# Second attention layer: the first mixture's outputs reach x by accumulating transfers from GpSimd

## The reference

```
x = x + graph_attention_0(layernorm(x), adj)      # 1 head
x = x + mixture_0(layernorm(x))                   # 8 experts, the best 2 of each token, weighted
x = x + graph_attention_1(layernorm(x), adj)      # 8 heads
x = x + mixture_1(layernorm(x))                   # 8 experts, the best 2 of each token, weighted
```

## Time and profile before

| | |
|---|---|
| median of 3 runs | 1700.94 us |
| the profiled execution's own time | 1694.58 us |
| its span | 1692.5 us |
| mean granted TensorE clock | 0.831 of full speed |
| last transfer issue of the first mixture, on GpSimd | 669.95 us |
| first work of the second attention layer, on GpSimd and SP | 675.76 us |
| first product with the neighbours, on TensorE | 752.47 us |

### The profile page before, as it was taken

The page is one execution under the profiler, slowest core; times in us unless marked ns, Lnnn a source line. Parts: engine busy times, 40 slices in busy tenths (PEclk is TensorE's granted clock), DMA queues, the critical chain, the costliest instruction groups (busy, mean ns, idle before and its releaser), DMA issues. The chain is left out here.

```text
span 1692.5 us, 31275 instructions
## 1 busy us (share of the span) xinstructions
PE 1099.7 (65%) x11083; PEld 1004.3 (59%) x11083; DVE 1103.8 (65%) x2450; ACT 1045.6 (62%) x1456; POOL 886.1 (52%) x694
## 2 busy tenths in 40 slices
PE   4677777731487672227777767777663169999960
PEld 3677677631376561127676667776663159999960
DVE  5689888762254441777989999999996224333424
ACT  5567766621365451059989999999981156666630
POOL 1011655686377776210312376776788626666660
PEclk9889977965699996558988898988886579999985
DMA  7654442112465550822221222322311355555528
GB/s 220 248 182 148 160 148 79 57 44 107 123 181 162 160 154 22 239 100 64 88 102 64 87 90 93 110 88 87 96 61 42 112 168 163 163 167 170 166 67 268
DMA packets 166122, 213.69 MB, mean 126 GB/s; under 512 B 29812, under 2 KB 121102, under 8 KB 164944
## 3 DMA queue, kind: packets, MB, share of 16 engines
q1 hardware_dynamic: 147792, 175.99, 33.8%
q0 software_dynamic: 18176, 35.72, 6.1%
HBM read 156.71 MB, written 58.56 MB: 127 GB/s over the span
## 5 line engine op out<-in xcount | busy, mean ns | idle before, releaser
L474 POOL DMA_INDIRECT y_dram<-f_ys,f_Xb x312 | 339.1, 1087 | 180.7 <-DVE f_ys L495 97.1
L1629 ACT ACTIVATE g_near<-g_s_row,g_steep 128x1024 fp8e4<-128x1024 f32 x400 | 420.9, 1138 | 17.0 <-issue 11.7
L185 POOL DMA_INDIRECT xs_dram<-r_row,r_pos x256 | 323.4, 1263 | 122.7 <-issue 77.2
L1573 PE MATMUL g_bp<-g_G,g_near 128*128 128x102 bf16 x4096 | 237.6, 228 | 151.1 <-DVE g_near L1439 151.0
L1573 PEld LDWEIGHTS g_bp<-g_G,g_near 128*128 128x128 fp8e4 x4096 | 229.7, 110 | 163.5 <-issue 163.3
L541 PEld LDWEIGHTS f_ops<-f_w,f_g 128*128 128x128 f32 x1872 | 239.9, 192 | 14.5 <-ACT f_g L577 0.7
L541 PE MATMUL f_ops<-f_w,f_g 128*128 128x128 f32 x1872 | 247.3, 275 | 0.1
L577 ACT ACTIVATE f_g<-f_hps,f_ex 128x512 f32<-128x512 f32 x234 | 160.8, 688 | 91.4 <-PE f_hps L533 91.1
L914 PE MATMUL attout<-V,Pt 128*128 128x129 f32 x1024 | 147.5, 305 | 28.4 <-DVE Pt L749 28.4
L1439 DVE TENSOR_TENSOR g_near<-g_near,g_mask 128x2048 uint32<-128x2048 uint32 x64 | 154.5, 2414 | 5.5 <-ACT g_near L1629 2.8
L914 PEld LDWEIGHTS attout<-V,Pt 128*128 128x128 f32 x1024 | 138.4, 217 | 29.7 <-DVE Pt L749 29.7
(11 more groups left out here) (237 smaller groups left out, 2107.3 us busy)
## 6 DMA issues: line engine op xcount, KB each, us to landing
raw<-in_adj SPq DMA_DIRECT2D x64, 512.0 KB, 6.2
g_s_row<-rows_dram SPq DMA_DIRECT2D x64, 512.0 KB, 3.8
f_Xb<-xs_dram SPq DMA_DIRECT2D x78, 288.0 KB, 3.0
f_w<-in_L_ffn_W SPq DMA_DIRECT2D x78, 256.0 KB
f_w<-in_L_ffn_W SPq DMA_DIRECT2D x78, 128.0 KB
mask_dram<-mask SPq DMA_DIRECT2D x16, 512.0 KB, 3.7
g_near<-y_dram SPq DMA_DIRECT2D x8, 1024.0 KB, 7.6
g_mask<-mask_dram SPq DMA_DIRECT2D x8, 1024.0 KB, 6.5
```

The costliest lines, as they stand in the source:

```text
L185: pool.indirect_dma_start(rows_d, bass.IndirectOffsetOnAxis(ap=pos[:, c % 2, k, t:t + 1], axis=0), row[:, c % RB, k, t, :], None, bounds_c ...
L474: pool.indirect_dma_start(y_d.rearrange("n k d -> (n k) d"), bass.IndirectOffsetOnAxis(ap=Xb[:, i % XB, r, D:D + 1].bitcast(U32), axis=0), ...
L1573: ins = pe.matmul(bp[h % 2][:, t // 4, (t % 4) * 6 * C:(t % 4 + 1) * 6 * C], near[:, k % 3, j, t * P:(t + 1) * P], G[:, s, j, h, :, :], st ...
L1629: ins = act.activation(near[:, k % 3, j, :], s_row[:, k % 3, :], ACT.Relu, scale=STEEP, bias=steep[:, s, j, h:h + 1], saturate=False)
```

## The change

The buffers for y, the eight loads and the sixteen sums on VectorE are gone, and so are the semaphore `s_add` and the waits for it. GpSimd issues two transfers for each batch, one for the first output and one for the second, which add what they read from `y_dram` to what is in `x_sb` (`accum_op=ALU.add`). The second of a batch waits for the first to land. VectorE's `take_moments(c)` waits until both have landed, and then does what the second half of `add_outputs(c)` did. Each batch has a semaphore of its own, `s_yl[c]`.

```diff
-            def load_outputs(b):
-                wait(sp, s_add, 2 * (b - 1))
-                sp.dma_start(yb[:, b % 2, :, :, :], y_d[b * N:(b + 1) * N, :, :].rearrange("(t p) k d -> p t k d", p=P)).then_inc(s_yl[b % 2], 16)
-
-            load_outputs(0)
-            load_outputs(1)
...
                     for h in range(4):
-                        if b == 0 and h == 1:
-                            for c in range(5, B):
-                                load_outputs(c)
                         load_row(b, h)
...
                 if b == -1:
-                    load_outputs(2)
-                    load_outputs(3)
                     R.sp_params(sp)
-                    load_outputs(4)
...
+            def add_first(c):
+                pool.dma_start(x_sb[:, c * NT:(c + 1) * NT, :], y_d[c * N:(c + 1) * N, 0, :].rearrange("(t p) d -> p t d", p=P), accum_op=ALU.add).then_inc(s_yl[c], 16)
+
+            def add_second(c):
+                pool.wait_ge(s_yl[c], 16)
+                pool.dma_start(x_sb[:, c * NT:(c + 1) * NT, :], y_d[c * N:(c + 1) * N, 1, :].rearrange("(t p) d -> p t d", p=P), accum_op=ALU.add).then_inc(s_yl[c], 16)
...
                 if b == -1:
-                    deviation(0)
+                    add_first(0)
+                    add_first(1)
+                    add_second(0)
+                    add_first(2)
                     R.pool_setup(pool)
-                    for c in range(1, B):
+                    for c in range(B):
+                        if c + 1 < B:
+                            add_second(c + 1)
+                        if c + 3 < B:
+                            add_first(c + 3)
                         deviation(c)
...
-            def add_outputs(c):
-                xb = x_sb[:, c * NT:(c + 1) * NT, :]
-                dve.wait_ge(s_yl[c % 2], 16 * (c // 2 + 1))
-                dve.tensor_tensor(xb, xb, yb[:, c % 2, :, 0, :], ALU.add).then_inc(s_add, 1)
-                dve.wait_ge(s_add, 2 * c + 1)
-                dve.tensor_tensor(xb, xb, yb[:, c % 2, :, 1, :], ALU.add).then_inc(s_add, 1)
-                dve.wait_ge(s_add, 2 * c + 2)
+            def take_moments(c):
+                dve.wait_ge(s_yl[c], 32)
...
-                hold(dve, (s_bp, k - 2), (s_add, 2 * B if k in (1, 2) else 0))
+                hold(dve, (s_bp, k - 2))
...
-                waits = [(s_row_ready[k % 3], (k // 3 + 1) * 16), (s_bp, k - 2), (s_add, 2 * B if k in (1, 2) else 0)]
+                waits = [(s_row_ready[k % 3], (k // 3 + 1) * 16), (s_bp, k - 2)]
```

More of the change, by code:

```diff
@@ L1143, in phase_gat1 @@
     y_d = K["y_dram"]
-    yb = near[:, 1:3, :, :].rearrange("p s t n -> p (s t n)").bitcast(FP32).rearrange("p (s t k d) -> p s t k d", s=2, k=2, d=D)
     Wext = T("Wext", [P, D + 2 * NH], FP32)
@@ L1181, in phase_gat1 @@
     s_c, s_w, s_ws, s_mask = S("c"), S("w"), S("ws"), S("mask")
-    s_add, s_st, s_m, s_var, s_rstd, s_xl, s_xp, s_xT, s_hp, s_hV = (S(n) for n in "add st m var rstd xl xp xT hp hV".split())
-    s_yl = [S(f"yl{i}") for i in range(2)]
+    s_st, s_m, s_var, s_rstd, s_xl, s_xp, s_xT, s_hp, s_hV = (S(n) for n in "st m var rstd xl xp xT hp hV".split())
+    s_yl = [S(f"yl{c}") for c in range(B)]
     s_lo, s_dg, s_mx, s_dM, s_nd, s_zf, s_zd, s_z, s_F, s_E, s_we = (S(n) for n in "lo dg mx dM nd zf zd z F E we".split())
@@ L1452, in step @@
                 if b == -1:
-                    add_outputs(0)
-                    add_outputs(1)
+                    take_moments(0)
+                    take_moments(1)
                     normalise_at(0, NORM)
@@ L1474, in step @@
                     if b == -1 and h < B - 2:
-                        add_outputs(h + 2)
+                        take_moments(h + 2)
                     if prepare:
```

## The result

The changed kernel takes 1716.0 us (median of 4; 1712.5 to 1718.3), the kernel before 1701.9 (median of 4). The ratio is 1.0091, with a 95% interval of 1.0055 to 1.0127. A second comparison (9 executions of the changed kernel, 26 of the kernel before) gave 1714.0 against 1701.6, ratio 1.0065, 1.0041 to 1.0090. So the change costs 0.7 to 0.9% (the two intervals together reach from 0.4 to 1.3%); 1717 us had been forecast. On the medians that is 14.1 and 12.5 us more.

What follows compares the result with a forecast made beforehand. VectorE set the opening before; afterwards the DMA engines' 16 x 3.2 + 18.9 = 70.1 us and 1.4 landing give +16.4, so 1700.9 + 16.4 = 1717 us. Own range 1711 to 1731; 8 in 10, 1700 to 1780.

Steps and rivals of the forecast that it cites:

- Two signs: Second attention layer's opening: batch 7's moments start near 748 us and TensorE's first neighbour product comes near 769 us.
- What bound the opening before: Start of the second attention layer, about 676 to 752 us: VectorE itself sets it, with 19.5 us of sums in its chain.
- (a) Moving the data: The sixteen transfers adding y into x: 3.2 us of DMA engine time each, for reading x as well as y.
- 18.9 us for the rest: DMA work in the opening that stays (parameters, mask, rows): 42.9 us less 24.0 us for the eight y loads.
- (b) Landing: Each accumulating transfer needs 1.4 us after its data to land, taken from the last store of x.
- (c) Issuing: GpSimd's issue of each 1024-row transfer takes 1 to 3 us.
- The rival of an issue growing in proportion with rows: GpSimd writes a descriptor per row, so each issue takes 7.8 us: +91 us (5 us each: +46); chance 0.23.
- The other loop: Opening's two-batch cycle of second transfer, landing, moments and power: 13.3 us, 6.7 a batch, beside 6.4 us of transfer.
- the other side: Rival for the sixteen transfers: accumulating costs no more than copying, 1.6 us each, giving 1695 us; chance 0.10.
- the cheap accumulation: Rival for the opening: transfers at copy cost, batch 7's moments 5.9 us sooner, spacing under 5.6 us as proof; chance 0.10.
- The slower accumulation: Rival for the sixteen transfers: slower than two passes, 5.4 us each, +52 us, 1752 us; chance 0.10.
- The signs: Checks in the profile: moments 6.5 to 9 us apart, landings 6 to 9 us after issue, attention changed by at most 2 us.

## Why the prediction was right

*The number:* it came nearer than the mechanism did, and that is partly luck. The forecast shift was 16.4 us; the medians moved by 14.1 and 12.5 us, the two openings by 10.1 and 12.1. Two signs that seem to be met exactly, batch 7's moments near 748 (748.29) and TensorE's first product near 769 (768.65), owe 6.1 us to the later start of the layer: counted from that start, the moments had been put at 72.7 us and came at 66.4 and 68.5. And the lower end of the range does not follow from its terms: 3.0 us a transfer gives 16 x 3.0 + 18.9 = 66.9 us of work and +13.2 us, 1714 us and not 1711.

*What bound the opening before:* right. VectorE waited for nothing from 685 to 737 us, and taking its sums away shortened the opening (by 10.0 us, no sums; by 5.1, copies from GpSimd).

*(a) Moving the data:* that the engines' work would bind held, and the size was a little high. I took two passes, 3.2 us for each transfer, between 3.0 and 3.6; measured were 2.88 where nothing else ran. 16 x 0.32 = 5.1 us of the 6.3 by which batch 7's moments moved less than forecast (10.1 against 16.4). The two profiles of the changed kernel differ by 2.0 us, so what remains, 1.2 us, is below what can be told. With the measured 2.88 us a transfer and 2.0 to land, and with the forecast's own 18.9 us for the rest and 1.2 before the first transfer, the sum gives 68.2 us for the moments that came at 66.4 and 68.5. It took the 18.9 us of other traffic as a constant beside the transfers, and that is not so in general: with 4 KB pieces, at nearly the same price of a transfer, the moments came at 55.6 us. What the accumulation in 512 B pieces costs is thus two things, the engines' time for the bytes and the small packets' weak stand against SP's queue, and the forecast priced only the first.

That the loss is the accumulation's own was shown by the copies, its packets included. The Trainium skill has a rule for the reducing step of a collective, that it reads twice on the same ring and runs at half the rate of a copy ("Collectives: The Full Stack", section "The bandwidth ceiling: the fold count and why AG ≠ RS ≠ AR"). Its figure fits here: 182 GB/s against the 349 GB/s of a load, a ratio of 1.9, and in 4 KB pieces 2.76 us against 1.48, the same ratio, though on two chips; against the 512 B copies (1.78) it is 1.55. That the reads are the cause was not tried.

*(b) Landing:* 1.4 us was taken. The quickest accumulating transfer landed 6.5 us after its issue began; 1.58 of issue and 2.88 of data leave some 2.0 us.

*(c) Issuing:* 1.58 us, inside the 1 to 3 taken (a first transfer's 2.25 us includes the end of the issue before it). The rival of an issue growing in proportion with rows, 7.8 us, falls: eight times the rows cost 1.8 times as much with accumulation (0.89 to 1.58).

*The other loop and the other side:* the cheap accumulation was forecast to bring batch 7's moments 5.9 us forward; with copies in its place they came 51.3 us after the start instead of 56.4, 5.1 us forward. So this rival's price was right, and only its condition was false. The slower accumulation (5.4 us) fell with 2.88.

*The signs:* not all of them were met. The moments of successive batches are 5.0 to 10.7 us apart, where 6.5 to 9 had been forecast, and the last step, 5.0 us, is below the 5.6 that was to prove the cheap accumulation, which 2.88 us rule out: one spacing was no test. Landings took 6.5 to 17.2 us, median 10.1, not 6 to 9. The attention, from the first to the last product with the neighbours, took 528.6 us before and 531.6 and 531.0 in the two profiles of the changed kernel, more than the 2 us that had been allowed; 531.7 with the first transfers up front, 529.0 to 530.4 in the other kernels on chips of this speed. The cause is open.

*What I had not foreseen:* that the piece size, through the packets, decides how the accumulating queue fares beside SP's small loads. It is as large as the measured loss: with 4 KB pieces, in a kernel that adds the wrong rows, the opening was no longer than before (76.0 against 76.7). Whether the small loads moved out of this stretch would give the same was not tried.

## What to carry to other kernels

An accumulating transfer is not a free sum: it cost 2.9 us of all DMA engines for 512 KB where half a load of 1024 KB is 1.5, so before moving sums to transfers, ask whether the DMA engines have as much idle time as the data need twice over, in that stage and not on average. When one engine is busy throughout a stage and the DMA engines at 0.74, relieving the first is worth only what the second leaves (here 10.0 us of 19.5), and each way of doing so must be priced on what it takes from the second. Pieces of 512 B that are added also went out as packets of 512 B and lost ground to another queue's small packets, which copied ones did not; if rows of a few KB can be had, have them first.

## What the hardware showed that I had not expected

- The same 8.39 MB in pieces of 512 B: 16640 packets when added, 2304 when copied.
- Beside a GpSimd sum of two inputs (2.3 us), VectorE's normalising of a batch took 4.2 us instead of 2.1 and an addition on 128 x 8 took 1.9 us instead of 0.17, while eight `bn_stats` took their usual 1.65.
- With SP's queue full of tiny loads, GpSimd's queue moved 0.84 MB in 6 us in added pieces of 512 B and 1.04 MB in added pieces of 4 KB, and the mask's landing on SP's queue went from 10.5 to 18.1 us.
- GpSimd's issue for 512 KB: 1.58 us accumulated in 1024 pieces, 0.89 in 128, 0.92 copied in 1024, 0.54 to 0.58 copied in 128.
- With all eight first transfers issued up front, the opening was 99.7 us against 86.8: batch 1's second transfer, issued at 697.73 us behind six firsts, was followed by its moments only at 722.57.
